# A new job table for a software-pipelined attention layer: k made in slots 4 and 6, other work and one store at other places, the prologue reordered

## What is computed

```python
x = x + 0.5 * ffn(layernorm(x))        # ffn: real(ifft(fft(x) @ w)) + bias
x = x + attention(layernorm(x))        # q, k, v = left @ W.T; softmax(q k / 4) v; @ Wo.T + bo
x = x + 0.5 * ffn(layernorm(x))
```

## Time and profile before

| what | value |
|---|---|
| median of 3 runs | 315.89 us (313.49 to 320.12) |
| the profiled execution | 312.38 us, its span 310.5 us |
| PE matmuls | 294.8 us busy, 95% of the span |
| ACT | 257.6 us, 83%, of which 256 exponentials 243.8 us |
| DVE | 190.5 us, 61% |
| POOL | 98.3 us, 32% |
| DMA | 49.33 MB, mean 159 GB/s |

### The profile page before, as it was taken

One profiled execution on the slowest core, in us unless ns is written; L12 is line 12 of the kernel. 1 busy time (PEld: TensorE's weight loads), 2 busy tenths in 40 slices (PEclk: granted clock), 3 DMA queues, 4 the chain that ended last, 5 costly groups with the idle time before them and its releaser, 6 DMA issues.

```text
span 310.5 us, 8810 instructions
## 1 busy us (share of the span) xinstructions
PE 294.8 (95%) x3440; PEld 112.5 (36%) x3443; DVE 190.5 (61%) x552; ACT 257.6 (83%) x285; POOL 98.3 (32%) x113
## 2 busy tenths in 40 slices
PE   8887999899998999999999999999999999998996
PEld 5633333233332333333333333334333333322333
DVE  1688546747775678657776678567755643370255
ACT  2117998898997889998998989998999999999921
POOL 6562531223604053223604251313600340034005
PEclk9999999999999999999999999999999999999999
DMA  7935615573462762665453663554372464112102
GB/s 192 337 137 192 218 65 153 195 270 133 139 217 83 245 208 103 208 204 217 155 192 129 231 205 112 198 172 143 131 238 104 138 205 170 38 68 70 37 34 70
DMA packets 25891, 49.33 MB, mean 159 GB/s; under 512 B 2032, under 2 KB 14192, under 8 KB 24048
## 3 DMA queue, kind: packets, MB, share of 16 engines
q1 hardware_dynamic: 25152, 48.26, 46.0%
q10 hardware_dynamic: 688, 0.40, 0.8%
HBM read 31.08 MB, written 17.56 MB: 157 GB/s over the span
## 4 chain that ended last, share of the span: by engine, by line
PE 75%; DMA 9%; DVE 5%; ACT 5%; issue 3%; POOL 3%; SPq 0%; ACTq 0%; POOLq 0%
PE ot L828 28%; PE misc L719 26%; PE scores L799 15%; ACT probs L669 5%; DMA leftT<-left_scr 4%; DMA q_scr<-qp 2%; PE scores L719 2%; DMA QS<-q_scr 2%; DMA left_scr<-left_blocks 1%; POOL x L553 1%; PE scores L686 1%; PE scores L693 1%; DVE left_blocks L966 1%; DVE lh L957 1%; POOL rstd L550 1%
## 5 line engine op out<-in xcount | busy, mean ns | idle before, releaser
L669 ACT ACTIVATE probs<-scores 128x1024 f32<-128x1024 f32 x256 | 243.8, 1028 | 20.6 <-PE scores L799 20.3
L828 PE MATMUL ot<-probs,VS 128*32 128x512 f32 x1024 | 133.9, 594 | 2.9 <-ACT probs L669 2.3
L799 PE MATMUL scores<-QS,KS 32*128 32x512 f32 x512 | 64.7, 495 | 3.0 <-DMA QS<-q_scr 1.3
L799 PEld LDWEIGHTS scores<-QS,KS 32*128 32x128 f32 x512 | 24.5, 181 | 109.8 <-ACT probs L669 101.0
L828 PEld LDWEIGHTS ot<-probs,VS 128*32 128x32 f32 x1024 | 30.6, 109 | 25.8 <-ACT probs L669 5.0
L563 POOL TENSOR_TENSOR x_out<-x,half_bias 128x512 f32<-128x512 f32 x7 | 9.0, 1292 | 88.8 <-DVE x L1012 88.8
L548 POOL TENSOR_SCALAR veps<-mv 128x4 f32<-128x4 f32 (+1 forms) x25 | 6.1, 242 | 95.9 <-DVE mv L946 95.9
L1017 DVE SCALAR_TENSOR_TENSOR x_out<-misc,rstd,x_out 128x256 f32<-128x256 f32 x28 | 13.5, 484 | 33.7 <-PE misc L719 30.2
L719 PE MATMUL misc<-half_ffn,xT 128*32 128x256 f32 x448 | 32.1, 386 | 0.0
L719 PE MATMUL misc<-half_ffn,xT_in 128*32 128x256 f32 x400 | 27.1, 385 | 1.4 <-DVE half_ffn L1193 1.3
L550 POOL TENSOR_TENSOR rstd<-veps,power 128x4 f32<-128x4 f32 (+1 forms) x25 | 25.3, 1013 | 2.1
(11 more groups left out here) (125 smaller groups left out, 260.0 us busy)
## 6 DMA issues: line engine op xcount, KB each, us to landing
KS<-k_scr SPq DMA_DIRECT2D x14, 512.0 KB, 4.9
QS<-q_scr SPq DMA_DIRECT2D x14, 512.0 KB, 4.6
x_in<-x SPq DMA_DIRECT2D x8, 512.0 KB, 5.1
xT_in<-x_t SPq DMA_DIRECT2D x8, 512.0 KB, 6.4
k_scr<-kp SPq DMA_DIRECT2D x8, 512.0 KB, 3.0
q_scr<-qp SPq DMA_DIRECT2D x8, 512.0 KB, 4.4
x_scr<-x_blocks SPq DMA_DIRECT2D x7, 512.0 KB, 2.9
xT<-x_scr SPq DMA_DIRECT2D x7, 512.0 KB, 4.7
```

What stands on the lines that cost most here:

```text
L669: nc.scalar.activation(probs[u % PRING][:, :, :], scores[u % SRING][:, :, :], ACT.Exp, scale=SCORE_SCALE).then_inc(exp_done, 1)
L799: last = mm(scores[(u + j // 2) % SRING][:, j % 2, :], KS[b % 2][rows, slot, kt * P:(kt + 1) * P].bitcast(F32R), QS[b % 2][rows, slot, :]. ...
L828: last = mm(ot[COL * j:COL * (j + 1), :], VS[b % 2][:, kt, h, :], probs[(u + j // 2) % PRING][:, j % 2, :], start=s % 8 == 0, stop=s % 8 == 7)
```

## The change

The table is new. In steady images k of image it+1 is made in slots 4 and 6 of image it, q in slots 8 and 9, v in 5 and 7, each beside half an F1 job in the other half of the bank; N moves from slot 10 to 11 and F2_3a from slot 0 of the next image to slot 15. Image 0 makes k of images 1 and 2, image 1 makes none, image 6 makes that of image 7. On DVE `normalize` of the first half moves from slot 12 to 9, `left_half` from slots 8 and 9 to 12 and 13, its turn to 14, the input stats from 11 and 13 to 6 and 8, the guard from 12 to 13. ACT's squares move from slots 4 and 10 to 8 and 11 (3 and 9 in image 1, 7 and 9 in image 6). SP issues q_out(1) before k_in(1), and in the loop k's and q's transfers together after those of x2. In the prologue POOL adds the first biases before the first rstd and computes rstd of image 0 in two parts, ahead of the last add of image 1; DVE normalises in two parts and takes the fourth F1 tile of image 1 after q; ACT makes `half_bias` earlier.

```diff
-          14: [("KT_0", 2, RIGHT)], 15: [("KT_1", 2, RIGHT)]}
+          4: [("KT_0", 1, RIGHT), ("F1_1a", 2, LEFT)], 5: [("F1_1", 2, LEFT), ("V_0", 1, RIGHT)],
+          6: [("KT_1", 1, RIGHT), ("F1_2a", 2, LEFT)], 7: [("F1_2", 2, LEFT), ("V_1", 1, RIGHT)], 8: [("QT_0", 1, RIGHT)],
...
             k_out(1)
+            q_out(1)
             k_in(1)
-            q_out(1)
             q_in(1)
             for it in range(1, B):
-                if it + 1 < B:
-                    k_out(it + 1)
                 if it >= 2:
                     store_out(it - 2, 1)
                 if it + 3 < B:
                     load_x(it + 3)
-                if it + 1 < B:
-                    k_in(it + 1, slice(0, 1))
                 x2_through(it - 1)
-                if it + 1 < B:
-                    k_in(it + 1, slice(1, None))
                 xT_in_from(it - 1)
                 if it + 1 < B:
-                    q_out(it + 1)
+                    k_out(it + 1)
+                    if it == B - 2:
+                        q_out(it + 1)
+                        k_in(it + 1)
+                    else:
+                        k_in(it + 1)
+                        q_out(it + 1)
+                    q_in(it + 1)
+                store_out(it - 1, 0)
                 if it + 2 < B:
                     left_through(it + 2)
-                if it + 1 < B:
-                    q_in(it + 1)
                 if it + 2 < B:
                     leftT_in(it + 2)
-                store_out(it - 1, 0)
...
-                    if s == (2 * 4 if it else 2 * 8):
+                    if s == (2 * 7 if it == B - 2 else 2 * 3 if it == 1 else 2 * 8):
                         square(kp, sq_k, kp_step, it + 1)
-                    if s == (2 * (8 if it == B - 2 else 10) if it else 2 * 9):
+                    if s == (2 * 11 if 1 < it < B - 2 else 2 * 9):
                         square(qp, sq_q, qp_step, it + 1)
```

More of the change, by code:

```diff
@@ L105, in slots_of @@
         ahead = [(f"F1_{t}", 2) for t in range(T)]
-        jobs = [(f"F1_{t}", 1) for t in range(T)] + [("LT", 1)] + ahead + [("KT", 1), ("QT", 1), ("N", 1)]
+        jobs = [(f"F1_{t}", 1) for t in range(T)] + [("LT", 1)] + ahead[:-1] + [("KT", 1), ("QT", 1), ahead[-1], ("N", 1)]
         return {s: [(name, d, LEFT)] for s, (name, d) in enumerate(jobs)}
@@ L127, in guard_slot @@
 def guard_slot(it):
-    return 12 if it else 13
+    return 13 if it < B - 2 else 12
 def evac_count(name, b):
@@ L321, in build_macaron @@
         rstd_done = [sem(f"rstd_done{i}") for i in range(3)]
+        ahead_biased = sem("ahead_biased")
+        first_stats = sem("first_stats")
+        first_mv = sem("first_mv")
+        first_veps = sem("first_veps")
+        first_rstd = sem("first_rstd")
         normed = sem("normed")
@@ L588, in _ @@
             add_row(x1[0], x_in[0], half_bias, early_biased, slice(1, 2))
+            rstd_of(0, 1)
             add_row(x1[0], x_in[0], half_bias, xb_done, slice(2, T))
             pool.wait_ge(x_loaded[1], 16)
-            add_rows(x1[1], x_in[1], half_bias, xb_done)
-            rstd_of(1, 1)
+            add_row(x1[1], x_in[1], half_bias, ahead_biased, slice(0, 2))
+            pool.wait_ge(first_mv, 1)
+            nc.gpsimd.tensor_scalar(veps[1][:, 0:2], mv[1][:, 0:2, 1], EPS, None, ALU.add).then_inc(first_veps, 1)
+            pool.wait_ge(first_veps, 1)
+            nc.gpsimd.tensor_tensor(rstd[1][0][:, 0:2], veps[1][:, 0:2], power[:, 0:2], ALU.pow).then_inc(first_rstd, 1)
+            rstd_of(1, 1, slice(2, T))
+            add_row(x1[1], x_in[1], half_bias, xb_done, slice(2, T))
             rstd_of(0, 2)
@@ L954, in left_half @@
             def left_half(b, tiles=range(T)):
-                dve.wait_ge(rstd_done[1], b + 1)
+                if b or tiles[-1] == T - 1:
+                    dve.wait_ge(rstd_done[1], b + 1)
                 for t in tiles:
@@ L1204, in _, with first_x1 @@
             fold(half_ffn, even[2], odd[:, :, :], ALU.subtract, ALU.add, 6, 4)
[L1205 to L1208, removed]
+            dve.wait_ge(mv_done[0], 1)
+            norm0_stats(1, range(0, 2))
+            def first_x1(t):
+                dve.wait_ge(evacuated, evac_count(f"F1_{t}", 0))
+                return nc.vector.bn_stats(stats[1][:, t, :], x1[0][:, t, :])
+            evacuate("F1_0", 0)
+            evacuate("F1_1", 0)
+            first_x1(0)
+            evacuate("F1_2", 0)
+            first_x1(1).then_inc(first_stats, 1)
+            dve.wait_ge(first_stats, 1)
+            for t in range(2):
+                last = nc.vector.bn_aggr(mv[1][:, t, :], stats[1][:, t, :])
+            last.then_inc(first_mv, 1)
+            evacuate("F1_3", 0)
+            first_x1(2)
+            first_x1(3).then_inc(stats_done[1], 1)
+            norm_moments(1, 1, range(2, T))
+            dve.wait_ge(first_rstd, 1)
+            left_half(0, range(0, 2))
+            norm0_stats(1, range(2, T))
+            left_half(0, range(2, T))
             norm_moments(0, 2)
-            run_jobs(PROLOGUE, T)
-            for t in range(T):
+            evacuate("LT", 0)
+            for t in range(T - 1):
                 evacuate(f"F1_{t}", 1)
-            run_jobs(PROLOGUE, 2 * T + 1)
-            run_jobs(PROLOGUE, 2 * T + 2)
+            evacuate("KT", 0)
+            evacuate("QT", 0)
+            evacuate(f"F1_{T - 1}", 1)
             dve.wait_ge(row_ready, 1)
             nc.vector.tensor_copy(KS[0][:, 0, :].bitcast(F32R), row_banks[0]).then_inc(first_k_set, 1)
-            run_jobs(PROLOGUE, 2 * T + 3)
+            evacuate("N", 0)
             for n, rows in ((2, KS[0][:, 1, :]), (3, QS[0][:, 1, :])):
```

49 lines of the change are left out of this document (25 added, 24 removed).

## The result

| | before | after |
|---|---|---|
| median | 313.85 us (6 runs, 310.23 to 320.12) | 315.83 us (6 runs, 314.14 to 321.88) |
| ratio, 95% interval | | 1.0109 [1.0066, 1.0152] |
| again, beside the experiments: median and ratio | 312.59 us | 316.24 us, 1.0104 [1.0049, 1.0158] |
| span of the execution read here | 310.5 us | 317.0 us |
| DVE busy | 190.5 us | 198.8 us |

The forecast was 1.8 us shorter; the kernel became 1.0 to 1.1% longer, some 3.3 us. The median of before is that of more runs than the prediction had, hence 313.85 and not 315.89. All rows of after come from an execution that took 318.78 us, 2.5 above the median of its kernel, so they show somewhat more loss than the medians do.

What follows compares the result with a forecast made beforehand. PE was taken to set the pace, each slot as long as its PE work. The terms summed to -1.8 us, 310.6 for the profiled execution, median 314.1; the 8 in 10 range was 310.8 to 318.5.

Steps and rivals of the forecast that it cites:

- prologue: Before the first score products: earlier biases, rstd and normalisation let PE turn the left half sooner; -1.0 us (-0.65 to -1.2).
- image 0: q stored ahead of k's loads removes PE's wait for QS, -1.4, and slot work changes by -0.1; together -1.5 us.
- image 1: Long slot loses its wait, -1.55; slot mix -0.64; q's square on ScalarE +0.5; together -1.7 us.
- images 2 to 5: PE's own work unchanged; small leftT wait -0.3, slot 8 wait +1.0, QS wait at slot 15 +1.2 us, all four images.
- image 6: Makes its own k: two empty slots become half, +0.44, and k's square costs +0.4; together +0.85 us.
- image 7: Slot 0 goes from full to half, less a little that ScalarE holds; -0.35 us (-0.43 to -0.1).
- The step that failed: DVE's moved normalisation, left half, input stats and guard cost nothing behind evacuations of slots 6, 8, 9, 12 to 14.
- leftT wait: PE's wait for left back from DRAM goes: image 1's long slot -1.55 us, images 2 to 5 -0.3 for all four.
- Slot 8: In images 2 to 5 the value product waits for DVE's later transpose: 0.27 each, some +1.0 us for four.
- The QS wait: In images 2 to 5 PE waits at slot 15 for q through DRAM: 0.3 each, +1.2 us; 0 to 1.9 per image.
- q late: Rival: slower store and load of q stop PE up to 1.9 us at slot 15, images 2 to 5; median 318.9; chance 0.17.
- The waits stay: Rival: PE still waits for QS in image 0 and leftT once, 1.4 and 1.5 us; median 317.0; chance 0.08.

Runs made afterwards that it cites:

- e12: Changed kernel plus two waits that put POOL's adds behind the left half, in the prologue and in the loop; 312.19 us, ratio 0.9957 to before.
- f2: f1 plus VectorE's slot 7 transpose of the attention output moved ahead of the F1 tile's sums; 310.64 us, ratio 0.9956 to before.
- a1: The changed kernel run again without any edit, beside the experiments; 316.24 us, ratio 1.0104 to before.
- f1: e12 plus q's store issued ahead of k's loads in SyncE's order in image 1 too; 311.74 us, ratio 0.9992 to before.
- p1: Kernel before plus only the change's reordered prologue and e2's wait; 311.73 us, ratio 0.9962 to before.
- b_one: Kernel before plus two idle POOL additions, one SBUF operand each, behind the rstd that releases lh in slot 8; 314.73 us, ratio 1.0078.
- e2: Changed kernel plus one wait: POOL's last prologue add to x1 of image 1 waits for the left half; 316.79 us, ratio 1.0107 to before.

## Why the prediction was wrong, step by step

PE's timeline cut as the prediction cut it, in us against the trace of before (the first line counts from the first F1 matmul to the first score products, image 7 to its slot 14):

| step | forecast | after | with both waits (e12) | f2 |
|---|---|---|---|---|
| prologue | -1.0 | -0.50 | -1.14 | -1.15 |
| image 0 | -1.5 | +2.35 | -1.13 | -0.94 |
| image 1 | -1.7 | -0.68 | -0.14 | -1.90 |
| images 2 to 5 | +1.9 | +3.96 | +1.38 | +0.34 |
| image 6 | +0.85 | +0.65 | +0.67 | +0.64 |
| image 7 | -0.35 | -0.35 | -0.35 | -0.35 |
| sum | -1.8 | +5.43 | -0.71 | -3.36 |

**The step that failed** is the last of the working: "The moved normalisation, left half, input stats and guard I cost at nothing: they stand on DVE behind the evacuations". I looked for room on DVE and found it, but never laid POOL's timeline beside DVE's at the new places. The cover was there; the instructions in it had grown from 0.59 to 2.24 and from 1.12 to 3.03. Taken out by e12, this step is worth 4.6 us in the medians, the whole distance between +3.3 and -1.3, and 4.4 in the traces, 1.05 of it the lower clock of a1's execution. With it removed the median does about what was forecast (312.19, 0.9957). Some of that is luck: the sum of e12's trace is -0.71; in it image 1 missed 1.56 of its 1.7, image 0 missed 0.37, and images 2 to 5 came out 0.52 better than their term.

**Prologue.** The mechanism was right, and with the add moved away it gave 1.15 where I had 1.0. In the change as made half of it was lost to the same hold: I put POOL's last add behind rstd in the sum as harmless, and it ran into the last two lh.

**Image 0.** The QS wait of slot 14 went, as forecast (3.28 to 1.93 in e12 and 1.87 in f1), and the hold brought 2.99 one slot earlier: 1.94 more of standing still and 1.05 at the lower clock.

**Image 1.** The leftT wait went, but a QS wait that I had not counted took part of its place (0.5 in a1, 1.7 in e12): I had worked out q's way through DRAM for images 2 to 5 and not for image 1, though the order on SP is the same there. Without it (f1, f2) the image gained 1.9, near the 1.7 forecast, but the parts differ: slot 14 gave 1.12 where 1.55 was forecast, the other slots 0.77 where the forecast had 0.64 less 0.5.

**Images 2 to 5.** Slot 8 was right: 0.25 to 0.31 each against 0.27, and f2 took it back. The leftT wait went. The QS wait was the right mechanism with a size that no single number has: slot 14 ran over its 2.29 by 0.07, 1.05, 0.70 and 1.61 in a1, against 0.3 each in the sum; in another execution of the same kernel the wait at image 5 alone was 3.2. In f1 it was absent, in f2 it came once with 0.8. The row of the table for these images compares single executions, and p1 shows that with before's own table one execution took 4 us longer there than another. Why the same program waits so differently from one execution to the next stays open, and so does why f1's median did not show the 1.8 us that its image 1 gained.

**Images 6 and 7** came out within 0.21 of their terms.

**The rivals.** None of them was the mechanism. *q late* was right in direction and for a part of images 2 to 5, and its sign, a wait for QS over 0.75, was there twice in a1 (0.91 and 1.53); but its place was second: with the hold gone and the queue as it was, e12 is faster than before. *The waits stay* falls: the old waits went.

## What to carry to other kernels

When an instruction of VectorE is moved, look at what GpSimd does at the new place, not only at whether VectorE has time there: a normalisation out of SBUF that takes 0.3 us alone took 1.3 where it met an addition of 128x512, since it ended only when the addition did. The cure was one semaphore wait on the engine that had time to spare. And where a transfer's way is worked out for the steady images, work it out for the first ones too, where the order of the queue is the same and the lead is not.

## What the runs showed of the hardware

- Which pairs hold: tensor_scalar out of SBUF and a tensor_tensor with two SBUF operands on DVE, beside tensor_tensor additions of 128x512 on POOL, are held until these end, within 0.1 us (0.59 to 2.24, 1.12 to 3.03, 0.36 to 2.41), one DVE instruction by each addition. Batch-norm stats were not (0.41 beside the adds and alone, a1). POOL's power (two operands too, but 128x4, 1.03 us) did not hold lh in e12: 1.09 at 54.80, while it ran from 54.19 to 55.22.
- A POOL instruction with one SBUF operand slowed the same lh and did not hold it for its whole length: 0.60 to 0.90 and 0.99 (b_one). Held for the whole of one such instruction (2.96 for two, 1.48 each), lh could not have ended before 118.74 + 1.48 = 120.22; it ended at 119.69. Here the rule of the Trainium skill, SBUF — State Buffer, section "SBUF: two separate sides", is stricter than the trace, for the same lh that the additions held.
- A stop of PE can be paid twice: in a1 2.25 us of idle time were followed by a stretch at granted clock 0.50, and the eight value products in it took from 60.39 to 62.25, 1.86, where e12's took 1.00. In e2 the same 2.25 at the same place were followed by a clock of 1.00. What decides between the two stays open.
